# Reading P1 of the next pair from PSUM before P3 of the present one, in a seven-product matrix pass

## What is computed

```
y     = einsum('bct,bcd->bdt', x, cond_weights[condition])        # 64 x 64 x 1024
base  = einsum('bsi,oi->bso', y, W_org)                           # 1024 -> 1024
q     = einsum('bi,ki->bk', y.mean(axis=1), Wq)
coef  = softmax(einsum('bk,ek->be', q, lora_keys) / sqrt(128))    # 8 experts
h     = einsum('bsi,eir->bser', y, lora_down)
delta = einsum('be,bser,ero->bso', coef, h, lora_up)
out   = x + base + delta
```

## Time and profile before

| | |
|---|---|
| median of 3 runs | 794.61 us (794.31 to 794.85) |
| the profiled execution | 793.19 us, of which the span shown is 791.4 us |
| TensorE (PE) busy | 719.7 us, 91% of the span |
| VectorE (DVE) busy | 491.8 us, 62% |
| ScalarE (ACT) busy | 237.6 us, 30% |
| GpSimd (POOL) busy | 165.2 us, 21% |
| DMA, mean over the span | 162 GB/s |

### The profile page before, as it was taken

How to read it: one execution, slowest core, us unless ns; L and a number is a source line. 1 busy time by engine, 2 the same in 40 slices (tenths; PEclk the granted TensorE clock), 3 DMA queues, 4 the chain that set the end, 5 groups by cost and what they waited for, 6 DMA issues and landing times.

```text
span 791.4 us, 10492 instructions
## 1 busy us (share of the span) xinstructions
PE 719.7 (91%) x3385; PEld 594.1 (75%) x3385; DVE 491.8 (62%) x757; ACT 237.6 (30%) x456; POOL 165.2 (21%) x141
## 2 busy tenths in 40 slices
PE   5697999999999999999995749999999999999997
PEld 4585887878878788787884637777777777777775
DVE  3579448374483744826445787776767677777673
ACT  4345235242351433514333431111111111111110
POOL 2431103012030020300200003322323232223232
PEclk9899999999999999999998969999999999999999
DMA  9952353344434434333321536666666666666642
GB/s 265 320 152 90 126 152 121 111 136 135 141 122 120 137 133 136 124 122 120 119 81 55 211 119 213 205 220 200 213 211 215 200 209 192 207 204 206 203 131 98
DMA packets 83672, 128.10 MB, mean 162 GB/s; under 512 B 18458, under 2 KB 51234, under 8 KB 81570
## 3 DMA queue, kind: packets, MB, share of 16 engines
q1 hardware_dynamic: 75024, 125.26, 48.6%
q10 hardware_dynamic: 8594, 2.17, 1.4%
HBM read 77.07 MB, written 50.33 MB: 161 GB/s over the span
## 4 chain that ended last, share of the span: by engine, by line
PE 73%; DVE 16%; issue 7%; DMA 1%; ACT 1%; POOL 1%; ACTq 1%; DVEq 0%; POOLq 0%; SPq 0%
PE x_ps L1282 21%; PE h_ps L1198 21%; PE w_ps L1282 10%; PE w_ps L1221 7%; PE y_ps L1176 6%; PE x_ps L1221 5%; DVE ba_l L760 4%; DVE blk L763 2%; DVE gs L763 1%; DVE tb_l L760 1%; DVE ga_l L760 1%; PE y_ps L1271 1%; DVE ysum L773 1%; DVE org_f L760 1%; DVE yg L791 1%
## 5 line engine op out<-in xcount | busy, mean ns | idle before, releaser
L459 POOL TENSOR_TENSOR blk<-blk,blkx 128x512 f32<-128x512 f32 x64 | 95.9, 1498 | 309.1 <-DMA blkx<-in_x_dram 155.6
L1282 PE MATMUL x_ps<-tb_h,ba_h 128*128 128x512 f32 x256 | 102.5, 400 | 29.5 <-DVE blk L763 28.4
L763 DVE TENSOR_TENSOR blk<-w_ps,blk 128x512 f32<-128x512 f32 x96 | 65.9, 687 | 61.3 <-PE w_ps L1282 32.5
L1198 PE MATMUL h_ps<-yq_h,down_h 128*128 128x512 f32 x256 | 101.8, 398 | 0.9 <-ACT ones_r L499 0.9
L1282 PE MATMUL x_ps<-tb_h,ba_l 128*128 128x512 f32 x256 | 100.3, 392 | 0.0
L1282 PE MATMUL x_ps<-tb_l,ba_h 128*128 128x512 f32 x256 | 100.2, 391 | 0.0
L1198 PE MATMUL h_ps<-yq_h,down_l 128*128 128x512 f32 x256 | 99.7, 390 | 0.0
L1198 PE MATMUL h_ps<-yq_l,down_h 128*128 128x512 f32 x256 | 99.7, 389 | 0.0
L843 DVE TENSOR_TENSOR g<-h_ps,coef 128x512 f32<-128x512 f32 x32 | 22.1, 691 | 117.7 <-PE h_ps L1198 98.3
L433 POOL TENSOR_TENSOR yq_l<-y_full,yq_h 128x512 fp32r<-128x512 f32 x32 | 46.3, 1448 | 198.7 <-ACT yq_h L499 198.7
L499 ACT ACTIVATE y_full<-y_ps 128x512 f32<-128x512 f32 x58 | 34.6, 597 | 163.3 <-PE y_ps L1176 163.3
(11 more groups left out here) (91 smaller groups left out, 1238.9 us busy)
## 6 DMA issues: line engine op xcount, KB each, us to landing
x_sb<-in_x_dram SPq DMA_DIRECT2D x32, 512.0 KB, 4.0
y_dram<-y_full SPq DMA_DIRECT2D x64, 256.0 KB, 2.7
r_dram<-blk SPq DMA_DIRECT2D x64, 256.0 KB, 2.4
yb<-y_dram SPq DMA_DIRECT2D x32, 512.0 KB, 7.5
blk<-r_dram SPq DMA_DIRECT2D x16, 1024.0 KB, 6.8
blkx<-in_x_dram SPq DMA_DIRECT2D x32, 512.0 KB, 6.9
out_dram<-blk SPq DMA_DIRECT2D x64, 256.0 KB, 4.0
x_sb<-in_L_ffn_W_org_dram SPq DMA_DIRECT2D x8, 512.0 KB, 3.8
```

The source lines that it names most:

```text
L459: pool.tensor_tensor(blk[p % 3][:, b, :], blk[p % 3][:, b, :], blkx[:, h, n, :], ALU.add).then_inc(x_added, 1)
L763: nc.vector.tensor_tensor(dst, a, b, ALU.add).then_inc(done, 1)
L1198: mm = nc.tensor.matmul(h_ps[:, m % 2, :], down[w][:, k, m * P:(m + 1) * P], yq[s][:, k, :], start=(k == 0 and i == 0), stop=(k == KC - 1 ...
L1282: mm = nc.tensor.matmul(bank, ba[s][n][:, k, :], tb[w][n][:, k, :], start=(first and k == 0 and i == 0), stop=(k == 3 and i == 2), skip_gr ...
```

## The change

In VectorE's list of work for the second pass, `take_b` of P1 leaves its place for all pairs but the first. For pairs 1 to 15 it stands one pair earlier in the list: behind the last operand preparation for pair `p + 1` (`b_lo_block` of P2) and ahead of `take_b` of P3 and `end_o21` of pair `p`. No instruction is added or removed, no wait is changed, and the other engines' lists are untouched.

```
                 if p > 0:
                     b_lo_sum(p, P6, 1)
                     b_lo_sum(p, P7, 2)
-                take_b(p, 0, P1, b1_ready)
+                if p == 0:
+                    take_b(p, 0, P1, b1_ready)
                 b_sum_4(p)
                 b_lo_sum(p, P5, 0)
                 end_o11(p)
...
                     b_sum_2(p + 1)
                     b_sum_3(p + 1)
                     b_lo_block(p + 1, P2, 0, 1)
+
+                    take_b(p + 1, 0, P1, b1_ready)
                 take_b(p, 1, P3, o12_ready)
                 end_o21(p)
```

## The result

The changed kernel takes 775.67 us (median of 4 runs, 774.48 to 776.29), the kernel before beside it 794.62. The ratio is 0.9757, 95% interval 0.9742 to 0.9773. The forecast was 775.6.

A forecast was written before the change was run, and what follows sets the result against it. TensorE was taken to bound the kernel, losing 1.27 us a pair waiting for VectorE's late take of P1 ahead of P6. 15 x 1.27 = 19.05 us off 794.61 gave 775.6 us, range 774.6 to 781.

The forecast's parts named there:

- The gap goes: TensorE ahead of P6, pairs 1 to 15: P6 follows P2 without a gap, 15 x 1.27 = 19.05 us off.
- the two bounds: Gain at P6: 1.12 us a pair if only the late start goes, 1.27 if the slow start goes too.
- P6's other operands leave 1.2 us: VectorE's low part of P6 ends at 606.6, P6's slot is 607.77: 1.2 us to spare in every pair.
- 2.34 us by an exclusive hold and 1.78 by the row: Low part of P1 meeting GpSimd's add: by the Trainium skill's lock P5 stalls 0.5 us a pair, by the profile row nothing.
- Take P3 is pushed back by 0.1 us under cover of the wait for P4: VectorE: take P3 starts about 602.6 instead of 602.53, covered by the 2.03 us wait for P4.
- Room of the `blk` load: The moved take's load lands at the latest at 608.4, the take comes at 621.0: room 12.6 us, nothing charged.
- The rival behind it: Slower: a late `blk` load holds the moved take at VectorE's head, 798 us at 17.6 us late; chance 0.04.
- its formula: `blk` load late: from 17.4 us on slower than the kernel before, by 15 us for each further us.
- Room of `yb`: Take P6 hangs on `yb` and is seen before P5's slot: room 1.18 us, 0.10 in the latest pair; nothing charged.
- Profile signs: P6 starts 19.04 to 19.1 us apart, 14 pairs about 267 us, VectorE's chain share from 16% to a few per cent.

The follow-up runs named there:

- 8 pairs: Against the kernel before, the take of P1 moved for the odd pairs alone, left at its old place for the even ones: 784.13 us, ratio 0.9876.
- the variants: Against the change, take of P1 placed later: behind `end_o21`, ahead of both low parts, 780.44 us; between the low parts of P6 and P7, 775.47 us.
- experiment 808: The change with each load of `blk` issued one pair later, behind the store of block 3; 808 us was expected, measured 836.68 us, ratio 1.0541.
- the later `yb`: The change with SyncE's two loads of `yb` issued behind the store of block 1 instead of ahead of it: 787.71 us, ratio 0.9918.
- the old order: The kernel before, take of P1 at its old place, with each load of `blk` issued one pair later: 794.28 us, ratio 1.0003.

## Why the prediction was right

- *The gap goes, 15 x 1.27 us.* Shown: 17.8 us over 14 pairs, and 10.4 us for 8 pairs (794.51 - 784.13), 1.30 each. Of the two bounds the upper one held; the slow first matmul went with the gap.
- *P6's other operands leave 1.2 us.* Shown, and the variants say what that rests on: the low part of P6 is out of GpSimd's way only because it is the first behind `end_o21`. With one instruction ahead of it 0.3 us a pair are lost. In the weighing of a low part that meets an add, 2.34 us by an exclusive hold and 1.78 by the row are no alternatives: the traces show an exclusive hold, and 1.78 us is what is left of it for a low part that comes 0.44 us after the add began.
- *Take P3 is pushed back by 0.1 us under cover of the wait for P4.* Shown: that wait went from 2.03 to 1.97.
- *Room of the `blk` load.* Not used up by the change. The rival behind it was under-priced. For a slip of one pair, 19.04 us, its formula gives 794.6 + 15 x (19.04 - 17.4) = 819 us and the expectation of the experiment 808; measured were 836.7. Where the expectation had 2.3 us a pair, P6 was 2.9 us late, with its low part behind GpSimd's add, and ran 1.4 us longer at the lower clock. The wait behind the add and the clock were both left out.
- *Room of `yb`, 1.18 us in the pair followed, 0.10 at least.* After the change take P6 is over at 604.68, seen 0.04 us later, and P5's slot is 600.38 + 5.44 = 605.82: 1.1 us. By the limit of 3.43 us found with the later `yb`, the smallest room in this execution was 0.05 us. One short wait of 0.2 us (of the weight loads) in it and one of 0.33 us in the other execution show that the smallest room is near zero indeed. That the prediction charged nothing for it held in the median.
- *Profile signs.* All came but one: VectorE's share of the chain is 11%, not a few per cent. The 16% of the earlier trace rows held its work of the first pass and for pair 0 too, which the change doesn't touch; the 5 points that went are those of the second pass.

## What to carry to other kernels

When a product accumulates onto a bank that another engine must first read, look at what stands ahead of that read in the reader's list, and put the read into the reader's last idle stretch before it is needed. Before moving it ahead of other work, measure the slack of everything that it waits for: the same move gave 19 us where its load was 12 us early, and lost 42 us against the old order where the load was late. Ask also which instruction ahead of the read holds it: here it would have been enough to pass one that the product did not need. A gain per period can be priced from the period less the unbroken pace, and then holds pair by pair.

## What the runs showed of the hardware

- An add of GpSimd and a VectorE instruction with two SBUF inputs don't run at the same time: the one that began first runs on, the other waits. In 12 of the 13 traces (all but that of 836.7 us), from 480 to 760 us, VectorE's instruction began during an add 310 times and ended 0.54 to 0.56 us behind the add's end each time, whatever its length (0.91 to 1.80 us, where it takes 0.68 alone). An add that began during such an instruction ended 1.13 to 1.17 us behind it in 320 of 325 cases, and so took up to 1.8 us instead of 1.29. A take with one input from PSUM kept its 0.69 us beside an add and did not hold it.
- With P6 2.0 to 3.5 us late in 14 pairs, the clock fell behind 12 of these waits: in the pair shown, granted clock 0.59 for 4.2 us behind 2.77 us of lateness, 1.7 us lost. The gaps of the kernel before, 0.96 us, left it at 1.00.
- Two executions of the changed kernel differed by 2.1 us: by 1.4 us at the start of the second pass, with a granted clock of 0.97 or 0.93 in the first 100 us, and by 0.6 us in one wait for `yb`.
